# Wide bf16 products for TensorE in the idle times of a top-k search, and ahead of the first list and the first rows

## The chip, the cores and the metric

The kernel runs on one core of one Trainium2 chip. The metric is the device time of one execution in microseconds (us); the profile is one execution on that core. TensorE's granted clock has two levels in these rows, 1.2 GHz (shown as 0.50) and 2.4 GHz (1.00).

## The reference

An input of 16 x 512 tokens of 256 channels goes through four residual layers: a Mamba layer, a mixture of experts (MoE), linear attention, and the same MoE again. The change touches only the MoE:

```python
scores = (x_flat @ Wg.T).T                               # 8 experts x 8192 tokens
top_vals, token_idx = jax.lax.top_k(scores, capacity)    # capacity = 8192 / 8 = 1024
token_w = jax.nn.softmax(top_vals, axis=-1)
xg = x_flat[token_idx]
h = jax.nn.silu(jnp.einsum('eic,ehc->eih', xg, W1)) * jnp.einsum('eic,ehc->eih', xg, W3)
y = jnp.einsum('eih,ech->eic', h, W2) * token_w[..., None]
out = jnp.zeros_like(x_flat).at[token_idx.reshape(-1)].add(y.reshape(-1, c))
```

So each expert takes the 1024 tokens that score highest for it.

## The kernel before

`moe` is called twice, as stage `f` and as stage `g`; the tiles of a stage carry its letter in front. Stages follow one another: every engine waits for `done` before it starts the next one. Each engine executes its own instructions strictly in the order in which its function issues them.

**Search.** The 8 x 8192 scores lie as 128 partitions of 512 (16 partitions to an expert). The threshold of each expert is found bit by bit in `ROUNDS` = 15 rounds, each of which settles two bits. In a round, VectorE (`count_round`) compares all scores with `PAIR` = 3 trial thresholds (three instructions, L1685, each adding one to the semaphore `above`) and prepares the next round's patterns (L1687). TensorE (`totals_of`) waits for each comparison in turn and adds up over the 16 partitions of an expert with eight products of 64 columns (L1564), whose fixed operand is the 128 x 128 bf16 matrix `blk_b`; the 24 products of a round go to `tot`, the first bank of the PSUM tile `yp`. After the last one VectorE reduces `tot` (L1690), compares the counts with 1024 (L1693) and makes the next three thresholds (L1697). Nothing of one round overlaps the next: it is a chain comparison, products, reduction, threshold.

**First list.** After the search come two marks and a few small fp32 products (L1585, L1587, L1589), two scans, and a transposition of the positions (L1593). VectorE makes the one-hot tiles of expert 0 (`hots`, L1630, L1637, L1642; ScalarE makes one more, L1417), TensorE `compact(0)` turns them into a token list with 64 small bf16 products (L1486, into the first bank of `tp`), ScalarE copies the sums out (L1423), `add_parts(0)` adds them (L1500), and VectorE writes the list `tok` (L1646, L1648).

**First rows.** GpSimd gathers the 1024 rows of expert 0 with eight indirect DMAs (L1377), four to each half. `transposes(0, 0)` waits for the first four and transposes them into the second bank of `tp`, `transposes(0, 1)` uses the first bank (L1514); ScalarE copies each out (L1430). Then `hidden(0)` starts its fp32 products of 512 columns (L1536), and from there TensorE is nearly always busy to the end of the stage.

The second bank of `tp` (`tp[:, 1, :]`) is first used by `transposes(0, 0)`. `blk_b` is written before the search (L1657), and TensorE waits for it ahead of the first round (`one` at 2). TensorE's order around the change is

```python
for r in range(ROUNDS):
    totals_of(r)
...
nc.tensor.matmul(mrow[:, 0:NE], one[:, 0:P], ind_sw[:], start=True, stop=True).then_inc(S["sw"], 1)
compact(0)
add_parts(0)
transposes(0, 0)
transposes(0, 1)
for e in range(NE):
    hidden(e)
```

Of the kernel before, what the change touches and what calls it, by code (L numbers as in the profile page):

```python
# [21 lines left out]
P = 128  # L22
# [4 lines left out]
TJ = T // P  # L27
# [1206 lines left out]
def moe(nc, done, name, xn, res, scores, w, by_pool, turn, cleared):  # L1234
# [13 lines left out]
    with ExitStack() as stack:  # L1248
# [7 lines left out]
        blk_b = s.sb("blk_b", [P, P], BF16)  # L1256
# [64 lines left out]
        tp = s.ps("tp", [P, 2, T])  # L1321
# [153 lines left out]
        def tensor(pe):  # L1475
            def compact(e):


                pe.wait_ge(S["hot"], e + 1)
                pe.wait_ge(S["lval"], e + 1)  # L1480
                pe.wait_ge(S["lpart"], e + 1)
                if e:
                    pe.wait_ge(S["xev"], max(e - 2, 0) * 4 + 4)
                for n in range(COLS):
                    q = n % 4
                    last = nc.tensor.matmul(tp[q * SB:(q + 1) * SB, 0, 0:NV * SB], hot[:, :, n],  # L1486
                                            val[:, n, :, :].rearrange("p v m -> p (v m)"),
                                            start=n < 4, stop=n >= COLS - 4, skip_group_check=True)
                last.then_inc(S["cp"], 1)

            def add_parts(e):


                pe.wait_ge(S["ev"], e + 1)
                if e:
                    pe.wait_ge(S["tok"], e)
                else:
                    pe.wait_ge(S["fold"], 1)
                for q in range(4):
                    last = nc.tensor.matmul(slot[q * SB:(q + 1) * SB, :], fold[:],  # L1500
                                            sums[:, :, q * NSLOT:(q + 1) * NSLOT], start=True, stop=True,
                                            skip_group_check=True)
                last.then_inc(S["fd"], 1)

            def transposes(e, g):
                q, k, half = e % 2, g % 2, g // 2
                if k == 0:
                    pe.wait_ge(S[f"g{q}{half}"], g_base + 16 * TJ * (e // 2 + 1))
                if g >= 2 or e and (g == 0 or e + 1 == NE):
                    pe.wait_ge(S["xev"], e * 4 + g - 1)  # L1510
                elif g == 1:
                    pe.wait_ge(S["ev"], e + 2 if e else 1)
                for j in range(TJ):
                    last = nc.tensor.transpose(tp[:, 1 - g % 2, j * P:(j + 1) * P],  # L1514
                                               xg[:, q, half * TJ + j, k * P:(k + 1) * P], ident[:])
                last.then_inc(S["tr"], 1)
# [37 lines left out]
            def total_of(r):  # L1554
                pe.wait_ge(S["cnt"], r + 1)
                nc.tensor.matmul(tot[:, 0:1], blk[:], cnt[:], start=True, stop=True).then_inc(S["tot"], 1)

            def totals_of(r):


                for v in range(PAIR):
                    pe.wait_ge(S["above"], r * PAIR + v + 1)
                    for j in range(0, T, PART):
                        last = nc.tensor.matmul(tot[:, v * PART:(v + 1) * PART], blk_b[:], above[:, v, j:j + PART, 1],  # L1564
                                                start=j == 0, stop=j + PART == T, skip_group_check=True)
                last.then_inc(S["tot"], 1)
# [9 lines left out]
                             start=True, stop=True).then_inc(S["mcol"], 1)  # L1576
# [4 lines left out]
            pe.wait_ge(S["one"], 2)  # L1581
            for r in range(ROUNDS):
                totals_of(r)
            pe.wait_ge(S["above"], ROUNDS * PAIR + 2)
            nc.tensor.matmul(tot[:, 0:1], blk[:], cg[:], start=True, stop=True).then_inc(S["tot"], 1)  # L1585
            pe.wait_ge(S["ldc"], 16 * len(later))
# [8 lines left out]
            pe.wait_ge(S["isw"], 1)  # L1595
            nc.tensor.matmul(mrow[:, 0:NE], one[:, 0:P], ind_sw[:], start=True, stop=True).then_inc(S["sw"], 1)

            compact(0)
            add_parts(0)
            transposes(0, 0)  # L1600
            transposes(0, 1)
            for e in range(NE):
# [15 lines left out]
        def vector(dve):  # L1618
# [157 lines left out]
            for e in range(NE):  # L1776
# [16 lines left out]
                if e + 2 < NE:  # L1793
                    slots(e + 2)
        return Stage(s, sync, gpsimd, scalar, tensor, vector)


# [938 lines left out]
```

## Time and profile before

| | us |
|---|---|
| median of 3 runs | 3231.95 (3231.19 to 3232.04) |
| the profiled execution | 3231.11 |
| its span, first to last instruction | 3229.3 |
| TensorE busy in the span | 2691.7 |
| the search of stage `f`, of stage `g` | 1766.4 to 1810.3, 2769.5 to 2813.4 |
| first product of `hidden(0)`, `f` and `g` | 1840.68, 2843.31 |

The mean granted clock of TensorE over the span is 0.898 of full speed. The profiled execution ran 1.8 us longer than its span. Times in the rows count from the start of the span. A row of the timeline is one instruction or a merged run of like ones (x24): start, the time that they cover together, engine, line, operation, output and inputs, and in brackets how long the engine idled before and what released it. PEld is a load of the fixed operand ahead of a product.

### The profile page before, as it was taken

How to read it: one execution, taken by the hardware profiler on the slowest of the kernel's cores; microseconds unless marked ns; L12 is line 12 of the kernel's file. 1: busy time of each engine (PE TensorE's matmuls, PEld its weight loads, DVE VectorE, ACT ScalarE, POOL GpSimd, SP SyncE). 2: the span in 40 equal slices, each digit the busy share in tenths (PEclk: the TensorE clock that was granted, in tenths of full speed). 3: DMA queues.
4: the chain of work that ended last, by engine and by line, in shares of the span. 5: the costliest groups of instructions: out<-in, count | busy, mean ns of one | idle time of the engine just before them, and what ended most of it. 6: DMA issues, size and time to landing. Idle time of an engine off the chain costs nothing.

```text
span 3229.3 us, 46992 instructions
## 1 busy us (share of the span) xinstructions
PE 2691.7 (83%) x16734; PEld 1452.3 (45%) x16734; DVE 2230.9 (69%) x2386; ACT 1801.4 (56%) x3170; POOL 2086.6 (65%) x1301
## 2 busy tenths in 40 slices
PE   7788878887887788877855599996999999479998
PEld 3234233333333233323323355663777777345565
DVE  3999999999999999999997622211666666532211
ACT  4777778778877877777763122222555554022221
POOL 3899999999999999999994044543334343043453
PEclk9889899888899888988876599998999999589999
DMA  5556655665566555665562023432111111223342
GB/s 145 121 122 141 149 136 128 139 159 124 132 143 147 142 133 133 142 149 137 122 141 80 16 67 86 92 60 55 39 49 55 55 48 48 63 51 77 84 92 26
DMA packets 225478, 325.18 MB, mean 101 GB/s; under 512 B 40705, under 2 KB 116993, under 8 KB 225122
## 3 DMA queue, kind: packets, MB, share of 16 engines
q1 hardware_dynamic: 200674, 288.09, 36.1%
q0 software_dynamic: 24576, 34.10, 6.3%
q8 instruction: 138, 2.26, 0.3%
q14 instruction: 90, 0.74, 0.1%
HBM read 236.11 MB, written 85.98 MB: 100 GB/s over the span
## 4 chain that ended last, share of the span: by engine, by line
PE 52%; DVE 20%; issue 8%; POOL 7%; ACT 6%; DMA 5%; SPq 1%; another core or an unknown queue 1%; DVEq 0%; POOLq 0%; ACTq 0%
PE t_wb L2301 9%; PE m_wk L912 9%; PE g_h L1536 7%; PE f_h L1536 7%; DVE m_pair L789 6%; DVE m_hc L789 4%; DMA m_bc<-bcd 4%; PE m_y L1009 4%; DVE m_hc L798 4%; PE g_yp L1550 3%; PE f_yp L1550 3%; POOL m_side L698 3%; POOL m_hc L707 2%; PE t_a_ps L2301 2%; PE t_num L2301 2%
## 5 line engine op out<-in xcount | busy, mean ns | idle before, releaser
L698 POOL TENSOR_TENSOR m_side<-m_du_r,m_bc 128x1024 f32<-128x1024 f32 x384 | 901.1, 2363 | 9.6 <-DMA m_du_r<-ddd 9.6
L707 POOL TENSOR_TENSOR m_hc<-m_hc,m_bc 128x1024 f32<-128x1024 f32 x224 | 527.8, 2359 | 116.7 <-DVE m_hc L789 115.6
L434 ACT ACTIVATE m_pair<-m_delta_r,m_a_neg 128x512 f32<-128x512 f32 x768 | 497.9, 680 | 179.7 <-DVE m_hc L798 93.7
L789 DVE TENSOR_TENSOR_SCAN m_pair<-m_pair,m_side 128x1024 f32<-128x1024 f32 x224 | 511.5, 2283 | 20.3 <-ACT m_pair L434 16.9
L1009 PE MATMUL m_y<-m_hc,m_fold 128*32 128x512 f32 x2048 | 324.6, 709 | 203.5 <-DVE m_hc L798 145.2
L789 DVE TENSOR_TENSOR_SCAN m_hc<-m_pair,m_side 128x1024 f32<-128x1024 f32 x160 | 362.8, 2276 | 9.9 <-ACT m_pair L434 5.4
L798 DVE TENSOR_TENSOR m_hc<-m_pair,m_bc 128x1024 f32<-128x1024 f32 x288 | 350.6, 1217 | 5.7
L912 PE MATMUL m_wk<-m_xnT,m_w_in 128*128 128x512 f32 x488 | 293.4, 732 | 23.3 <-DVE m_delta L774 23.3
L912 PE MATMUL m_wk<-m_xs,m_cw_diag 128*128 128x512 f32 x480 | 226.8, 605 | 10.1 <-ACT m_xs L504 10.1
L1536 PE MATMUL g_h<-g_xgT,g_w 128*128 128x512 f32 x512 | 223.8, 597 | 0.8 <-issue 0.8
L1782 DVE TENSOR_TENSOR g_hT<-g_sg,g_h 128x512 f32<-128x512 f32 x64 | 44.0, 688 | 260.9 <-ACT g_sg L1445 260.9
L1782 DVE TENSOR_TENSOR f_hT<-f_sg,f_h 128x512 f32<-128x512 f32 x64 | 44.0, 688 | 260.6 <-ACT f_sg L1445 241.1
L1536 PE MATMUL f_h<-f_xgT,f_w 128*128 128x512 f32 x512 | 223.4, 596 | 0.8 <-ACT f_xgT L1430 0.8
L458 ACT ACTIVATE m_prod<-m_du_t,m_b_t 128x256 f32<-128x256 f32 x512 | 215.5, 496 | 3.1 <-PE m_pair L1065 2.2
L1009 PEld LDWEIGHTS m_y<-m_hc,m_fold 128*32 128x32 f32 x2048 | 45.6, 115 | 368.0 <-issue 367.9
L1377 POOL DMA_INDIRECT f_xg<-xn,f_tok x64 | 64.3, 1005 | 213.7 <-DVE f_tok L1648 196.7
L1377 POOL DMA_INDIRECT g_xg<-xn,g_tok x64 | 64.0, 1000 | 213.7 <-DVE g_tok L1648 196.6
L912 PEld LDWEIGHTS m_wk<-m_xnT,m_w_in 128*128 128x128 f32 x488 | 99.8, 227 | 217.3 <-issue 165.2
L789 DVE TENSOR_TENSOR_SCAN m_hc<-m_side,m_pair 128x1024 f32<-128x1024 f32 x64 | 146.0, 2282 | 38.2 <-issue 21.4
L434 ACT ACTIVATE m_side<-m_delta_r,m_a_neg 128x512 f32<-128x512 f32 x256 | 167.8, 711 | 0.0
L1065 PE MATMUL m_pair<-m_ident,m_prod 128*128 128x128 f32 x1024 | 139.7, 281 | 24.3 <-DVE m_hc L798 16.7
L1065 PEld LDWEIGHTS m_pair<-m_ident,m_prod 128*128 128x128 f32 x1024 | 120.6, 146 | 85.2 <-issue 85.2
(339 smaller groups left out, 4962.0 us busy)
## 6 DMA issues: line engine op xcount, KB each, us to landing
m_delta_r<-ddd SPq DMA_DIRECT2D x252, 256.0 KB, 6.6
m_du_r<-ddd SPq DMA_DIRECT2D x252, 256.0 KB, 7.5
m_bc<-bcd SPq DMA_DIRECT2D x192, 128.0 KB, 3.0
ddd<-m_delta SPq DMA_DIRECT2D x31, 512.0 KB, 3.0
ddd<-m_du SPq DMA_DIRECT2D x31, 512.0 KB, 3.8
f_w<-in_w SPq DMA_DIRECT2D x24, 512.0 KB
g_w<-in_w SPq DMA_DIRECT2D x24, 512.0 KB
m_xt<-in_x SPq DMA_DIRECT2D x16, 512.0 KB, 9.9
```

Of the source, the lines that this page charges most:

```text
L434: last = nc.scalar.activation(to, delta_r[:, c % 2, q, :], ACT.Exp, scale=a_neg[:, c * NQ + q, st:st + 1])
L458: last = nc.scalar.activation(prod[:, :, :, k, n * SB:(n + 1) * SB], du_t[:, k, :, :].rearrange("p c (h f d) -> p (c h) f d", h=2, d=SB), ...
L698: nc.gpsimd.tensor_tensor(side[:, un % RING, :, :], du_r[:, c % 2, 2 * h:2 * h + 2, :], bc[:, 0, st:st + 1, :].to_broadcast([P, 2, T]), AL ...
L707: nc.gpsimd.tensor_tensor(hc[:, un % RING, :, :], hc[:, un % RING, :, :], bc[:, 1, st:st + 1, :].to_broadcast([P, 2, T]), ALU.mult).then_i ...
L789: nc.vector.tensor_tensor_scan(to, decay, added, 0.0, ALU.mult, ALU.add).then_inc(S["scan"], 1)
L798: nc.vector.tensor_tensor(hc[:, un % RING, :, :], pair[:, un % 2, :].rearrange("p (i t) -> p i t", t=T), bc[:, 1, st:st + 1, :].to_broadca ...
L912: return nc.tensor.matmul(out, lhsT, rhs, start=first, stop=last)
L1009: last = nc.tensor.matmul(y[q * SB:(q + 1) * SB, c % 2, :], fold[:], hc[:, (2 * m + q // 2) % RING, q % 2, :], start=False, stop=st == NSE ...
L1065: last = nc.tensor.transpose(pair[:, un % 2, f * T + k * P:f * T + (k + 1) * P], prod[:, c % 2 * 2 + h, f, k, :], ident[:])
L1536: last = nc.tensor.matmul(out[:, m % 2, :], wt[:, q, k, f * P:(f + 1) * P], xgT[:, q, k, half * T:(half + 1) * T], start=k == 0, stop=k == ...
L1550: last = nc.tensor.matmul(yp[:, l % 2, 0:C], hT[:, half, f, j * P:(j + 1) * P], w2[:, e % 2, f, :], start=f == 0, stop=f == KF - 1)
L2301: return nc.tensor.matmul(out, lhsT, rhs, start=first, stop=last, **kw)
```

## The change

A function `unread(n)` is added to TensorE's part of `moe`. It issues n products of 512 columns in bf16: the fixed operand is `blk_b`, the moving operand is `blk_b` read four times over, and the output is the second bank of `tp`, which nothing reads before `transposes(0, 0)` overwrites it. No product waits for a semaphore or raises one. `unread(5)` follows the 24 products of each of the 15 rounds, `unread(12)` stands ahead of `compact(0)`, and `unread(16)` between `add_parts(0)` and `transposes(0, 0)`. That is 15 x 5 + 12 + 16 = 103 products in a stage, 206 in all. No other engine's instructions change.

```diff
+            def unread(n):
+                wide = blk_b[:].rearrange("p (o c) -> p o c", o=1).to_broadcast([P, TJ, P])
+                for _ in range(n):
+                    nc.tensor.matmul(tp[:, 1, :].rearrange("p (o c) -> p o c", c=P), blk_b[:], wide, start=True, stop=True)
+
             for r in range(ROUNDS):
                 totals_of(r)
+                unread(5)
...
+            unread(12)
             compact(0)
             add_parts(0)
+            unread(16)
             transposes(0, 0)
             transposes(0, 1)
```

## Rows read from the trace of the kernel before

**Rows 1.** Groups by line, the search: xcount | busy us, mean ns | idle before.

```profile
L1564 PE MATMUL f_yp<-f_junk,f_blk_b 128*128 128x64 bf16 x360 | 21.9, 242 | 20.1 <-DVE f_junk L1685 20.1
```

**Rows 2.** Timeline, one round of stage f.

```profile
1805.39 1.28 DVE L1685 TENSOR_SCALAR f_junk<-f_sc,f_trial 128x512 f32<-128x512 f32 x3
1805.93 1.30 PEld L1564 LDWEIGHTS f_yp<-f_junk,f_blk_b 128*128 128x128 bf16 x24 [1.59 <-DVE f_junk L1685]
1805.94 1.46 PE L1564 MATMUL f_yp<-f_junk,f_blk_b 128*128 128x64 bf16 x24 [1.43 <-DVE f_junk L1685]
...
1807.43 0.36 DVE L1690 TENSOR_REDUCE f_count<-f_yp 128x3 f32<-128x192 f32 x1 [0.69 <-PE f_yp L1564]
...
1808.28 1.28 DVE L1685 TENSOR_SCALAR f_junk<-f_sc,f_trial 128x512 f32<-128x512 f32 x3
```

**Rows 3.** Windows: length, busy us (count) by engine, granted clock, DMA share, GB/s.

```profile
core 0: us, PE busy (x) PEld busy (x) DVE busy (x) ACT busy (x) POOL busy (x), PEclk, DMA share, GB/s
452.00:461.00 9.00, 5.92 (x36) 2.81 (x36) 8.97 (x5) 7.54 (x14) 8.56 (x6) 1.00 0.31 117
461.00:470.00 9.00, 5.89 (x40) 2.87 (x44) 8.93 (x6) 6.37 (x12) 8.03 (x4) 1.00 0.78 193
...
478.50:481.80 3.30, 1.12 (x9) 0.31 (x10) 3.27 (x3) 2.58 (x6) 3.30 (x2) 1.00 0.26 66
482.00:485.20 3.20, 3.20 (x4) 0.68 (x2) 3.17 (x3) 2.36 (x5) 3.20 (x3) 0.50 0.45 142
...
1768.00:1810.00 42.00, 21.95 (x362) 19.68 (x361) 29.30 (x112) 0.58 (x1) 0.00 (x0) 0.50 0.22 53
1810.00:1820.00 10.00, 2.24 (x14) 1.92 (x12) 7.76 (x18) 0.00 (x0) 0.00 (x0) 0.50 0.00 0
...
1840.60:1843.90 3.30, 3.22 (x4) 1.51 (x5) 0.00 (x0) 1.24 (x1) 0.44 (x1) 0.50 0.26 73
1844.00:1855.00 11.00, 11.00 (x33) 5.39 (x32) 5.37 (x6) 3.45 (x6) 0.00 (x0) 1.00 0.00 0
...
2843.30:2847.20 3.90, 3.89 (x5) 1.82 (x6) 0.00 (x0) 1.16 (x1) 0.42 (x1) 0.50 0.22 62
```

**Rows 4.** One line, L1500: duration ns min/median/max, first and last start us.

```profile
L1500 PE MATMUL f_yp<-f_sums,f_fold x32: 182/183/196, 1829.3 to 2111.4; 128*32 128x16 bf16 x32
```

**Rows 5.** Timeline of stage f behind the search.

```profile
1812.65 0.59 PE L1585 MATMUL f_yp<-f_cg,f_blk 128*128 128x1 f32 x2 [2.36 <-DVE f_eq L1711]
...
1813.10 0.56 PE L1587 MATMUL f_h<-f_ce,f_low 128*128 128x1 f32 x2
...
1816.76 0.59 PE L1589 MATMUL f_h<-f_rows,f_low 128*128 128x1 f32 x2 [3.09 <-DVE f_sel L1723]
...
1819.65 1.11 PE L1593 MATMUL f_yp<-f_ident,f_pos 128*128 128x128 f32 x4 [2.30 <-DVE f_pos L1730]
...
1821.78 0.59 PE L1596 MATMUL f_yp<-f_ind_sw,f_one 128*128 128x8 f32 x2 [1.02 <-DVE f_ind_sw L1754]
...
1825.14 2.29 DVE L1642 TENSOR_TENSOR f_val<-f_lhot,f_tileb 128x2048 bf16<-128x2048 bf16 x1
...
1827.53 1.47 PE L1486 MATMUL f_tp<-f_val,f_hot 128*32 128x64 bf16 x64 [5.15 <-DVE f_val L1642]
...
1829.32 0.20 PE L1500 MATMUL f_yp<-f_sums,f_fold 128*32 128x16 bf16 x4 [0.32 <-ACT f_sums L1423]
...
1837.95 1.97 PE L1514 MATMUL f_tp<-f_ident,f_xg 128*128 128x128 f32 x8 [8.42 <-DMA f_xg<-xn,f_tok]
...
1840.68 8.69 PE L1536 MATMUL f_h<-f_xgT,f_w 128*128 128x512 f32 x16 [0.77 <-ACT f_xgT L1430]
```

**Rows 6.** Timeline, the same kinds of product at 2.4 GHz, later in stage f.

```profile
1860.47 1.66 PE L1486 MATMUL f_tp<-f_val,f_hot 128*32 128x64 bf16 x64
...
1877.01 0.66 PE L1514 MATMUL f_tp<-f_ident,f_xg 128*128 128x128 f32 x4 [1.96 <-DMA f_xg<-xn,f_tok]
```

**Rows 7.** Timeline, loads for `hidden(0)` as the clock rises.

```profile
1843.38 0.34 PEld L1536 LDWEIGHTS f_h<-f_xgT,f_w 128*128 128x128 f32 x1 [0.52 <-issue]
1844.06 0.19 PEld L1536 LDWEIGHTS f_h<-f_xgT,f_w 128*128 128x128 f32 x1 [0.34 <-issue]
1844.49 0.19 PEld L1536 LDWEIGHTS f_h<-f_xgT,f_w 128*128 128x128 f32 x1 [0.24 <-issue]
```

## The prediction

> **What bounds the kernel now.** I read the groups by line first, to see what TensorE does in the search. It is busy 21.9 us and idles 20.1 us, always until a comparison of VectorE is there [rows 1]. The timeline of one round comes next, because an average can't tell which half of the chain is late [rows 2]. A round lasts 2.89 us (1805.39 to 1808.28). The three comparisons take 1.28; TensorE starts 0.55 behind their start and ends at 2.01 (1807.40); VectorE then needs 0.88 for reduction and threshold before the next comparison. So TensorE's tail, 0.73 us from the end of the comparisons to the end of the products, lies on the path in each round, and VectorE waits 0.69 us for it. Third, the windows give the granted clock. Through the search, where TensorE is busy half the time, it is 0.50, that is 1.2 GHz; it stays there until `hidden(0)` has been dense for 3.3 us in stage f and 3.9 us in g, and is 1.00 behind [rows 3]. The 24 products are a queue at this clock: they cover 1.46 us, the last one alone takes 0.242, so they start every 0.053 us, which is 64 columns at 1.2 GHz. That is what can shrink. The added products compute nothing; their only possible gain is the clock.
>
> **A wide product's price.** None is in the trace. By the 0.053 us of 64 columns, 512 columns take eight times as long, 0.427 us at 1.2 GHz, and half of it, 0.213, at 2.4. Five take 2.13 or 1.07 us, twelve 5.12 or 2.56, sixteen 6.83 or 3.41.
>
> **Do they raise the clock?** In the first round they start behind the last small product, at about 1769.6, and at 1.2 GHz run to 1771.7. The next round's first comparison is there at 1771.2, so TensorE goes straight on, without a gap. This is the situation of the start of `hidden(0)`: dense work, and the clock up 3.3 and 3.9 us later [rows 3]. I expect the rise at 1772 to 1775, in the second or third round. **Do they hold it?** In a warm round TensorE works for 24 x 0.027 + 1.07 = 1.7 of 2.63 us, 65%, with one gap of 0.5 to 0.6 and two small ones. The stretch 452 to 470 of the Mamba stage is busy 11.8 of 18 us, 66%, with longer gaps, all at 1.00; a fall came behind 478.5 to 481.8, busy 1.12 of 3.30 [rows 3]. So I take it as held to the end of the search.
>
> **A warm round.** The third comparison is ready at 1.35 us after the round's start (comparisons start 0.40 apart, and TensorE follows 0.55 behind the first). The products of the first two are then out of the way, since eight take 8 x 0.027 = 0.21, under 0.40. The end is at 1.35 + 7 x 0.027 + the duration of one product. That duration is 0.242 cold. How much of it scales is bounded by the 16-column product, 0.196 in the cold stretch and 0.183 warm: nearly all of it is fixed, so 64 columns take 0.205 to 0.215 warm [rows 4]. End: 1.75 instead of 2.01, **0.26 us saved in a warm round**. The spacing of 0.027 is no row for a 128-column load with each product. Bounds: 0.053 (nothing changes) and 0.026, which the 64 products of `compact` show at 2.4 GHz (1.66 us) [rows 6]. I take the lower, as fp32 loads shorten with the clock, 0.34 to 0.19 us [rows 7]. The warm wide products end about 1.54 + 1.07 + 0.03 = 2.6 us after the round's start, and the next round's small ones are not due before 2.63 + 0.55 = 3.18: they are hidden, with 0.5 us of room.
>
> By the Trainium skill, "TensorE: Matmul & The Clock Gate", section on single matmul latency, an isolated product takes (219 + N)/1.2 ns cold and (398 + N)/2.4 ns warm, which for 64 columns is 236 and 192. The trace agrees with the first (242) and shows no second. As an estimate by that page a warm round would save 0.28 and the two stages together 0.5 us more than my sum.
>
> **The cold rounds.** There the cover fails. The five run to 1771.7 against 1771.2, so the second round ends 0.5 us late; if the clock has not risen in its wide products either, the third loses another 0.5, because 24 small and 5 wide ones take 1.28 + 2.13 = 3.41 us, more than 2.89. I take 0.5 with a quarter of a chance of 1.0, and a small chance of less if the rise comes early: 0.5. Sum for one search: 13 warm rounds x 0.26 = 3.4, less 0.5, is **2.9 us**; 12 rounds less 1.0 gives 2.1, 14 rounds with hardly a loss 3.5.
>
> **Behind the search.** The last five are done 1.1 us after the last small product, well ahead of L1585 (2.4 behind it). That product and L1587 take 1.0 us together at 1.2 GHz; if the clock is still up, 0.6 to 0.7. After that TensorE does 2.24 us of work in 10 [rows 3, 5], and the clock falls somewhere. Gain 0 to 0.8 (with L1589 and the four transpositions, 1.11 cold against 0.66 warm [rows 5, 6]); I take 0.3.
>
> **`unread(12)`** starts when L1596 is through, at 1822.25 in times of before. All cold it ends at 1827.4, and `compact(0)` is released at 1827.5 by VectorE [rows 5]: a cover with 0.1 us of room. If the clock rises on the way there is more. Cost 0 to 0.1; I take 0. `compact(0)` itself gains nothing from the clock: 64 products cover 1.47 us cold and 1.66 warm [rows 5, 6]. So this edit is worth -0.2 to 0, and I take 0.
>
> **`unread(16)`** starts at 1829.5 and ends at 1833.0 warm, 1836.4 cold; the rows are there at 1837.9 [rows 5]. It is hidden by the gather, with 1.5 us of room at least. Does its warmth reach the rows? Behind it TensorE idles 1.5 to 4.9 us. The stretch with 1.12 us of work in 3.3 was followed by a fall [rows 3], so in most phases the clock falls ahead of `hidden(0)` or within it. What is to be had: the transpositions, 1.97 us against at most 1.3 (twice the 0.66 of four), so 0.6 or more [rows 5, 6]; and four to five products of `hidden(0)` that ran at half speed for 3.3 and 3.9 us, that is 1.65 and 1.95 us. What is to be lost: a rise a little later than in this execution, up to 1.5. I take +0.3.
>
> **Sum.** 2.9 + 0.3 + 0 + 0.3 = 3.5 us a stage, 7.0 in all. Everything from `tok` on is a chain through gather and transpositions, and TensorE is dense behind it, so the gain isn't given back later. The profiled execution took 3231.11, 0.84 less than the median; so much is what two rises that come a little early or late make. Against it the sum gives 3224.1, against the median 3224.95. I forecast **3224.8 us**, a ratio of 0.998.
>
> **The rivals.**
> *Warm to the end of the gather* (R1): the clock is still up when `hidden(0)` starts, in both stages. For: the gap is only 1.5 us if `unread(16)` runs mostly cold. Against: if it does, it rose late, and warm it leaves 4.9. It adds 0.6 to 2.3 a stage: about 3221.
> *The rounds don't shorten* (R2): the clock rises, but a product with its 128-column load keeps starting every 0.053 us. For: no row shows such a pair warm. Against: loads scale in fp32 [rows 7]. The products then are a queue of 24 as before, and a round ends at 0.55 + 23 x 0.053 + 0.21 = 1.98 against 2.01: it saves 0.03 us, 0.4 a search, less 0.5, plus 0.6 behind it. Time 3231 to 3232, no change.
> *The clock does not rise, or not for long* (R3, the other side): the wide products then run at 1.2 GHz, each round becomes 24 small and 5 wide back to back, 3.41 us, and loses 0.52. In 14 rounds 7.3 us a stage: 3246. It decides as soon as more than 5 of 14 rounds are cold, for 5 x 0.52 = 2.6 then meets 9 x 0.26 = 2.3. For: these operands are bf16 with most values zero, and no dense stretch of such products is in the trace; the small ones ran half busy through 42 us without a rise. Against: both dense starts of `hidden(0)` and that of 482 to 485 ended in a rise [rows 3].
>
> **Chances.** Forecast 0.67 (its own range 3222.5 to 3227.5), R1 0.12, R2 0.12, R3 0.06, of which a partial one of 3230 to 3240 is half; 0.03 for anything else. The range of 8 in 10 takes in R1 and the lesser sizes towards R2: 3220.0 to 3230.0. A measurement of this kernel tells about 0.2%, 6.5 us, from no change; that line is at 3225.5, inside the forecast's own range. Two thirds of the forecast (0.44) and all of R1 lie beyond it: faster 0.56. Same 0.37, from the rest and R2. Slower 0.07.
>
> **What would show it.** In the windows of both searches the clock goes from 0.50 to 1.00 within 7 us and stays. A warm round in the timeline lasts 2.63 us, its 24 products cover 1.2, and VectorE waits 0.4 instead of 0.69. The second round, alone or with the third, is longer than 2.89. `compact(0)` starts right behind L1642, the first transposition waits for the gather's DMA and not for TensorE. If the rounds last 3.4, it is R3; if they last 2.87 at a clock of 1.00, R2; if `hidden(0)` shows no half-speed product, R1. I am wrong if the clock falls between rounds, or if `unread` stands in the way of `compact(0)` or of the rows.

## The result, and the profile after

The change takes **3223.8 us** (median of 14 runs, 3219.6 to 3226.4), the kernel before on the same chips 3231.36 (14 runs, 3229.7 to 3233.3). The ratio is 0.9977, 95% interval 0.9969 to 0.9984. Forecast were 3224.8 us (range 3220.0 to 3230.0) and a ratio of 0.998.

The groups by line, stage `f`, of the changed kernel (L1571 is L1564 of before, the small products; L1695 is L1685, a comparison; L1700 is L1690, VectorE's reduction; L1563 are the added products; idle time stands behind the second bar):

```profile
L1563 PE MATMUL f_tp<-f_blk_b 128*128 128x512 bf16 x103 | 28.6, 420 | 0.0
...
L1571 PE MATMUL f_yp<-f_junk,f_blk_b 128*128 128x64 bf16 x360 | 18.4, 199 | 4.6 <-DVE f_junk L1695 4.6
...
L1700 DVE TENSOR_REDUCE f_count<-f_yp 128x3 f32<-128x192 f32 x15 | 5.4, 357 | 8.7 <-PE f_yp L1571 8.7
```

The 360 small products took 242 ns each before [rows 1] and take 199 now, and TensorE idles 4.6 us ahead of them instead of 20.1. Being busier is no gain in itself; the gain is that VectorE's reduction waits 8.7 us in its 15 rounds. Before it waited 11.8: 0.69 in each round [rows 2] but the first, which cost 2.05 in both kernels, because TensorE still has four fp32 transpositions to do there.

Where the clock was, in stretches of stage `f` of the changed kernel (columns as in [rows 3]):

```profile
1771.00:1774.20 3.20, 3.20 (x30) 1.80 (x27) 2.09 (x8) 0.00 (x0) 0.00 (x0) 0.50 1.02 388
1774.40:1811.00 36.60, 31.08 (x392) 16.51 (x389) 29.09 (x111) 0.00 (x0) 0.00 (x0) 1.00 0.13 14
1811.00:1815.00 4.00, 0.61 (x4) 0.52 (x4) 3.34 (x8) 0.00 (x0) 0.00 (x0) 1.00 0.00 0
1815.20:1820.30 5.10, 1.79 (x8) 1.30 (x9) 4.13 (x12) 0.00 (x0) 0.00 (x0) 0.51 0.00 0
1820.30:1825.40 5.10, 5.10 (x13) 1.62 (x13) 5.07 (x3) 2.00 (x1) 0.00 (x0) 0.50 0.00 0
1825.60:1831.00 5.40, 5.08 (x84) 2.86 (x84) 0.33 (x2) 0.21 (x1) 1.85 (x2) 1.00 0.07 15
1831.00:1835.60 4.60, 0.06 (x1) 0.00 (x0) 2.63 (x6) 0.00 (x0) 3.38 (x5) 1.00 0.36 104
1835.80:1838.50 2.70, 1.97 (x8) 1.57 (x8) 0.00 (x0) 1.17 (x2) 2.09 (x3) 0.51 0.42 108
1838.60:1842.50 3.90, 3.88 (x5) 1.83 (x6) 0.00 (x0) 1.18 (x1) 0.43 (x1) 0.50 0.21 60
1842.70:1852.00 9.30, 9.30 (x29) 4.56 (x28) 4.71 (x4) 2.16 (x4) 0.00 (x0) 1.00 0.00 0
```

Read as a story: the search starts at 1.2 GHz; behind 3 us of dense work the clock is up, and it stays up to the end of the search. Behind it TensorE does 0.61 us of work in 4 and the clock falls. `unread(12)`, from 1820.3, runs at half speed, and the clock is up again just as it ends, at 1825.6. `unread(16)` runs at full speed and is done at 1831.0; TensorE idles 4.8 us, the clock falls at 1835.8, and the first rows arrive at 1835.9. So the transpositions and 4.0 us of `hidden(0)` run at half speed; before, it was the transpositions and 3.3 us. From the timeline:

```profile
1820.31 5.28 PE L1563 MATMUL f_tp<-f_blk_b 128*128 128x512 bf16 x12
...
1835.89 1.97 PE L1514 MATMUL f_tp<-f_ident,f_xg 128*128 128x128 f32 x8 [4.83 <-DMA f_xg<-xn,f_tok]
```

The first rounds and a later one, from the timeline of the changed kernel:

```profile
1770.02 1.49 PE L1571 MATMUL f_yp<-f_junk,f_blk_b 128*128 128x64 bf16 x24
...
1771.32 2.32 PE L1563 MATMUL f_tp<-f_blk_b 128*128 128x512 bf16 x5
...
1772.39 1.28 DVE L1695 TENSOR_SCALAR f_junk<-f_sc,f_trial 128x512 f32<-128x512 f32 x3
...
1773.44 1.31 PE L1571 MATMUL f_yp<-f_junk,f_blk_b 128*128 128x64 bf16 x24
...
1775.64 1.28 DVE L1695 TENSOR_SCALAR f_junk<-f_sc,f_trial 128x512 f32<-128x512 f32 x3
...
1799.34 1.28 DVE L1695 TENSOR_SCALAR f_junk<-f_sc,f_trial 128x512 f32<-128x512 f32 x3
...
1799.88 1.20 PE L1571 MATMUL f_yp<-f_junk,f_blk_b 128*128 128x64 bf16 x24 [0.35 <-DVE f_junk L1695]
...
1800.92 1.24 PE L1563 MATMUL f_tp<-f_blk_b 128*128 128x512 bf16 x5
1801.12 0.36 DVE L1700 TENSOR_REDUCE f_count<-f_yp 128x3 f32<-128x192 f32 x1 [0.43 <-PE f_yp L1571]
...
1801.97 1.28 DVE L1695 TENSOR_SCALAR f_junk<-f_sc,f_trial 128x512 f32<-128x512 f32 x3
```

In the second round the products start 1.05 us behind the comparison (1773.44 against 1772.39) instead of 0.55: the five wide ones at 1.2 GHz were in the way, and the round lasts 3.25 us (1772.39 to 1775.64). The warm round lasts 2.63 (1799.34 to 1801.97) instead of 2.89 [rows 2].

To compare kernels I cut each stage into six parts at instructions of its timeline and take differences of their starts. *Search*: first comparison to the first mark (L1710 of before). *Marks*: to the first ranks (L1738). *List*: to `tok` (L1648). *Gather*: to the first transposition. *Transp.*: to the first product of `hidden(0)`. *Hidden*: to the second step of VectorE's products there (L1782). Microseconds, stage f / stage g:

| kernel | search | marks | list | gather | transp. | hidden | sum |
|---|---|---|---|---|---|---|---|
| before | 44.74 / 44.75 | 9.63 / 9.62 | 8.98 / 8.96 | 8.17 / 7.73 | 2.73 / 2.74 | 9.36 / 9.80 | 83.61 / 83.60 |
| the change | 41.71 / 41.75 | 9.01 / 9.01 | 8.87 / 8.92 | 8.14 / 7.79 | 2.73 / 2.49 | 9.78 / 10.08 | 80.24 / 80.04 |

The change saves 3.37 and 3.56 us, 6.9 together, by this cut. The two spans differ by less, 4.8 us, mainly because what stands ahead of the first search, and is not changed, ran longer in that execution: the first comparison came at 1768.16 instead of 1766.43. A single span is no measure of a change of this size; the cut by stage and the medians are.

### The profile page after: what moved, and what is told of

Same layout as the page of the kernel before. It is cut to its first block, busy times and chain, and to the rows that moved or that the text cites. A ratio compares the mean times of both kernels' runs of the same rounds, so it can differ in the third digit from the quotient of the medians.

```text
span 3224.5 us, 47404 instructions
## 1 busy us (share of the span) xinstructions
PE 2735.5 (85%) x16940; PEld 1458.2 (45%) x16940; DVE 2230.9 (69%) x2386; ACT 1801.9 (56%) x3170; POOL 2086.3 (65%) x1301
## 4 chain that ended last, share of the span: by engine, by line
PE 52%; DVE 19%; issue 9%; POOL 7%; ACT 6%; DMA 5%; SPq 1%; another core or an unknown queue 1%; DVEq 0%; POOLq 0%; ACTq 0%
PE t_wb L2311 9%; PE m_wk L912 9%; PE g_h L1536 7%; PE f_h L1536 7%; DVE m_pair L789 6%; DVE m_hc L789 4%; DMA m_bc<-bcd 4%; PE m_y L1009 4%; DVE m_hc L798 4%; PE f_yp L1550 3%; PE g_yp L1550 3%; POOL m_side L698 3%; POOL m_hc L707 3%; PE t_a_ps L2311 2%; PE t_num L2311 2%
```

## The experiments

All ratios are to the kernel before on the same chip. The experiments ran on chips where it takes 3216 to 3218 us in place of 3231, so only ratios and the cut are compared. Lines shift by a few between these kernels; the comparison is L1693 in e3 and e4, and the small and the wide products keep L1571 and L1563.

| kernel | median us | ratio, 95% interval |
|---|---|---|
| e1_search_only | 3209.32 | 0.9977 (0.9968 to 0.9986) |
| e2_lists_only | 3216.67 | 0.9998 (0.9989 to 1.0008) |
| e3_two_wide | 3213.91 | 0.9991 (0.9982 to 1.0000) |
| e4_eight_wide | 3209.72 | 0.9978 (0.9968 to 0.9988) |
| e5_three_wide | 3209.91 | 0.9980 (0.9971 to 0.9989) |
| e6_thirty_four | 3204.67 | 0.9965 (0.9952 to 0.9979) |
| e7_gaps_filled | 3205.37 | 0.9965 (0.9952 to 0.9979) |
| e8_three_early_filled | 3204.73 | 0.9969 (0.9958 to 0.9981) |
| e9_change_again | 3209.69 | 0.9975 (0.9966 to 0.9984) |
| e10_early_then_five | 3201.74 | 0.9953 (0.9940 to 0.9967) |

| kernel | search | marks | list | transp. | hidden | sum |
|---|---|---|---|---|---|---|
| e1 | 41.54 / 41.23 | 9.13 / 9.21 | 8.96 / 8.93 | 2.74 / 2.73 | 9.59 / 9.56 | 80.06 / 79.41 |
| e2 | 44.74 / 44.73 | 9.62 / 9.62 | 8.96 / 8.89 | 2.73 / 2.37 | 10.51 / 10.20 | 84.71 / 83.50 |
| e3 | 42.15 / 42.95 | 9.62 / 9.62 | 8.94 / 8.96 | 2.73 / 2.73 | 10.15 / 9.23 | 81.79 / 81.23 |
| e4 | 42.23 / 42.36 | 9.21 / 9.21 | 8.96 / 8.93 | 2.73 / 2.74 | 9.22 / 9.50 | 80.48 / 80.43 |
| e5 | 41.10 / 41.10 | 9.20 / 9.61 | 8.96 / 8.93 | 2.74 / 2.74 | 9.20 / 9.31 | 79.35 / 79.46 |
| e6 | 41.89 / 41.76 | 9.20 / 9.01 | 8.97 / 8.89 | 1.91 / 1.91 | 7.78 / 7.77 | 77.94 / 77.11 |
| e7 | 41.54 / 41.12 | 8.55 / 8.54 | 8.91 / 8.93 | 1.92 / 1.92 | 7.77 / 7.77 | 76.90 / 76.04 |
| e8 | 41.10 / 41.10 | 8.75 / 8.75 | 8.94 / 8.94 | 1.92 / 1.91 | 7.77 / 7.77 | 76.60 / 76.19 |
| e9 | 41.59 / 41.86 | 9.10 / 9.21 | 8.92 / 8.91 | 2.73 / 2.49 | 9.73 / 10.07 | 80.01 / 80.28 |
| e10 | 41.10 / 41.11 | 8.55 / 8.55 | 10.06 / 8.90 | 1.91 / 1.91 | 7.77 / 7.77 | 77.57 / 76.03 |

(The gather is 7.7 to 8.2 us in every kernel and left out.)

### Which of the three places carries the gain

```diff
 e1_search_only, against the change
-            unread(12)
...
-            unread(16)
```

> Only the five products a round; the 12 and the 16 are left out. Theory: the gain is the shorter rounds of the search and a little behind it. Search of a stage (first comparison to the marks) 41.7 us as with the whole change (44.75 before), marks 9.0, list and gather as before; time 3224 to 3226, no more than 1 us from the whole change. Rival (the 12 and the 16 carry a warm clock to the list and the rows and share the gain): 3226 to 3228.

```diff
 e2_lists_only, against the change
-                unread(5)
```

> Only the 12 ahead of the first list and the 16 ahead of the first rows. Theory: both are hidden and bring nothing; search 44.75, list 8.9 to 9.0 us, the clock is back at 1.2 GHz for part of the transpositions and of hidden(0); time 3230 to 3232. Rival: a warm clock reaches hidden(0), 1.6 to 2.5 us a stage, 3226 to 3228.

The search alone gives the whole ratio, 0.9977; the 12 and the 16 alone give 0.9998, which is no measurable change. In e2 the search stays at 44.74 and 44.73. Its windows for stage `f` show the 12 and 16 working and their work lost (1.00 from 1824 to 1833, then 0.50 again as the rows come):

```profile
1824.00:1831.00 7.00, 5.29 (x85) 2.96 (x84) 1.16 (x3) 0.75 (x2) 2.18 (x2) 1.00 0.08 22
1831.00:1833.00 2.00, 0.00 (x0) 0.00 (x0) 1.71 (x4) 0.00 (x0) 1.66 (x2) 1.00 0.42 104
1834.00:1843.00 9.00, 6.93 (x14) 3.76 (x15) 0.00 (x0) 2.46 (x3) 3.50 (x4) 0.50 0.28 75
```

The hidden part is even longer, 10.51 and 10.20 us against 9.36 and 9.80. So two of the three edits of the change are worth nothing that can be measured, as sized.

### How many wide products a round needs

```diff
 e3_two_wide and e4_eight_wide, against e1_search_only
-                unread(5)
+                unread(2)    # e3; unread(8) in e4
```

> Two wide products a round in place of five, and no 12 and 16. At 1.2 GHz a round then has 1.28 + 0.85 = 2.13 us of work in 2.89, with an idle time of 0.7 us in each. Theory (the clock rises only behind dense work, and it is the clock that shortens the rounds): it stays at 0.50 through the search, rounds last 2.89, search 44.75, time 3230 to 3232. Rival (any more work in the idle time does it, without a late second round): the clock is 1.00, search 41.1, time 3224.

Both theories missed. The clock does rise with two, in the second round of both stages, but it doesn't stay. Windows of e3, stage `f`:

```profile
1770.00:1780.00 10.00, 6.36 (x104) 3.56 (x101) 7.84 (x32) 0.00 (x0) 0.00 (x0) 1.00 0.60 100
1780.50:1786.00 5.50, 4.50 (x52) 2.68 (x50) 3.90 (x16) 0.00 (x0) 0.00 (x0) 0.50 0.00 0
1787.00:1793.00 6.00, 4.00 (x66) 2.16 (x62) 4.52 (x17) 0.00 (x0) 0.00 (x0) 1.00 0.00 0
1794.00:1800.00 6.00, 4.79 (x56) 2.99 (x57) 4.39 (x17) 0.00 (x0) 0.00 (x0) 0.50 0.00 1
```

It goes up and down with the same instructions in each round, and the rounds follow it. Timeline of e3, a round in front of a rise and one behind it:

```profile
1782.71 1.28 DVE L1693 TENSOR_SCALAR f_junk<-f_sc,f_trial 128x512 f32<-128x512 f32 x3
1783.25 1.46 PE L1571 MATMUL f_yp<-f_junk,f_blk_b 128*128 128x64 bf16 x24 [0.57 <-DVE f_junk L1693]
...
1785.60 1.28 DVE L1693 TENSOR_SCALAR f_junk<-f_sc,f_trial 128x512 f32<-128x512 f32 x3
1786.15 1.20 PE L1571 MATMUL f_yp<-f_junk,f_blk_b 128*128 128x64 bf16 x24 [0.58 <-DVE f_junk L1693]
...
1788.24 1.28 DVE L1693 TENSOR_SCALAR f_junk<-f_sc,f_trial 128x512 f32<-128x512 f32 x3
```

At 1.2 GHz the round lasts 2.89 us and its 24 products cover 1.46; at 2.4 GHz it lasts 2.64 and they cover 1.20. The instructions are the same, so it is the clock that shortens a round, and not the mere presence of the wide products. My premise that only gapless work raises it was wrong: here it rose from rounds with an idle 0.6 us in each. The search gains 2.6 and 1.8 us, and the two stages differ by 0.8 with the same code.

> Eight wide products a round in place of five, and no 12 and 16. Theory: only the rounds before the clock rises pay, since eight at 1.2 GHz take 3.41 us; warm, they end 0.1 us behind the first comparison of the next round, which the slack of the first two comparisons takes up, so a warm round stays at 2.63. Search 42.5 to 43.5, time 3225.5 to 3228. Rival (a wide product that ends behind the first comparison costs its overhang in every round): search 44 to 45, time 3229 to 3231.

The theory held: with eight, a warm round is still 2.64 us (1790.43 to 1793.07), although its products start 0.68 us behind the comparison instead of 0.54. Timeline of e4:

```profile
1790.43 1.28 DVE L1693 TENSOR_SCALAR f_junk<-f_sc,f_trial 128x512 f32<-128x512 f32 x3
1791.11 1.07 PE L1571 MATMUL f_yp<-f_junk,f_blk_b 128*128 128x64 bf16 x24
1792.02 1.89 PE L1563 MATMUL f_tp<-f_blk_b 128*128 128x512 bf16 x8
...
1793.07 1.28 DVE L1693 TENSOR_SCALAR f_junk<-f_sc,f_trial 128x512 f32<-128x512 f32 x3
```

Only the products of the third comparison set the end, and they find TensorE free. What eight cost is the second round, with the clock still down (3.76 and 3.88 us): search 42.2 and 42.4 in place of 41.1 to 41.9 with five. That is 0.1 to 0.3 us under the lower end I had given; the ratio, 0.9978, can't tell eight from five.

```diff
 e5_three_wide, against e1_search_only
-                unread(5)
+                unread(3)
```

> Three wide products a round, and no 12 and 16. At 1.2 GHz a round has 1.28 + 1.28 = 2.56 us of work in 2.89, so that the next one's products are not late. Theory (three raise the clock and hold it, and the late second round of the change is saved): search 41.0 to 41.4 us in both stages, clock 1.00 from the second or third round to the end, 0.2 to 0.7 us less than with five; ratio to before 0.9973 to 0.998. Rival (three are like two, where the clock went up and down): search 42 to 43, clock falls between rounds, ratio 0.9985 to 0.999.

Of two, three, five and eight, three is the best size for the search: 41.10 us in both stages, the clock up from the second round and held, no round late. Windows of e5:

```profile
1772.00:1808.00 36.00, 25.52 (x372) 14.17 (x370) 28.42 (x111) 0.00 (x0) 0.00 (x0) 1.00 0.15 22
2756.00:2761.00 5.00, 3.93 (x33) 2.72 (x33) 2.78 (x12) 1.31 (x2) 0.00 (x0) 0.50 1.02 398
2762.00:2798.00 36.00, 25.17 (x365) 13.84 (x362) 28.46 (x111) 0.00 (x0) 0.00 (x0) 1.00 0.15 19
```

The change's 41.7 is 0.6 longer: the price of its second round, 3.25 and 3.28 us against 2.63. With five that price depends on when the clock rises: the second round of the other kernels with five lasts 2.65 (e7, stage `g`) to 3.41 us (e6, stage `f`). The ratios, 0.9980 in e5 and 0.9977 in e1 and in the change, can't tell these sizes apart.

### Why the 16 ahead of the first rows brought nothing

```diff
 e6_thirty_four, against the change
-            unread(16)
+            unread(34)
```

> The whole change with 34 wide products ahead of the first rows in place of 16. Theory (the clock fell because TensorE idled 4.8 us before the first rows): 34 take 7.3 us warm and end 1 us before the rows, the clock is 1.00 at the transpositions and in hidden(0); transpositions 2.1 us to the first product of hidden(0) instead of 2.5 to 2.7, the first two steps of hidden(0) 7.7 instead of 9.4 to 10.1; 2 to 2.5 us less a stage than the change, ratio 0.9960 to 0.9968. Rival (products for transpositions and hidden(0) start at half speed whatever runs before): no difference from the change, 0.9977. A third case: the 12 have not raised the clock, the 34 start cold and delay the rows, gather 1 to 4 us longer.

The theory held, by the cut and by the ratio, 0.9965. Timeline of TensorE in e6, stage `f`:

```profile
1825.51 7.51 PE L1563 MATMUL f_tp<-f_blk_b 128*128 128x512 bf16 x34
1834.02 1.09 PE L1514 MATMUL f_tp<-f_ident,f_xg 128*128 128x128 f32 x8 [1.00 <-DMA f_xg<-xn,f_tok]
1835.93 7.11 PE L1536 MATMUL f_h<-f_xgT,f_w 128*128 128x512 f32 x16 [0.82 <-ACT f_xgT L1430]
```

The eight transpositions cover 1.09 us instead of 1.97, and the 16 products of `hidden(0)` 7.11 instead of 8.69 [rows 5]. One number, an idle time of 1.0 instead of 4.8 us ahead of the rows, makes transpositions and hidden part 2.8 and 2.9 us shorter than in the change (9.69 and 9.68 against 12.51 and 12.57).

### Filling every gap

```diff
 e7_gaps_filled, against the change
 nc.tensor.matmul(offp[:, 0:1], low[:], ce[:], ...)
+            unread(10)
...
 nc.tensor.matmul(mcol[:, 0:1], low[:], rows[:], ...)
+            unread(7)
...
-            unread(12)
+            unread(22)
...
-            unread(16)
+            unread(34)
```

> The whole change, and TensorE filled at 2.4 GHz from the search on: 10 wide products behind L1595, 7 behind L1597, 22 ahead of the first list, 34 ahead of the first rows. Theory: the clock, up since the search, stays at 1.00 to the end of the stage; marks 8.4 us in place of 9.0, list 8.9, transpositions 2.1, first two steps of hidden(0) 7.7; 2.8 to 3.3 us less a stage than the change, ratio 0.9955 to 0.9962. Rival: the added ones stand in the way where each gap is short, marks 9.0 or more, and the gain over the change is under 2 us a stage.

From 1782 to 1855, in stage `f`, the clock is 1.00 in every window. The cut says 3.3 and 4.0 us less than the change, a little more than expected. The ratio, 0.9965, is above the range I gave (0.9955 to 0.9962), and it can't tell this kernel from e6.

```diff
 e8_three_early_filled, against e7_gaps_filled
+            pe.wait_ge(S["one"], 2)
+            unread(2)              # ahead of total_of(1)
...
+            unread(2)              # ahead of the transpositions of ex
...
-                unread(5)
+                unread(3)
```

> As e7_gaps_filled, but three wide products a round in place of five, and two each in two idle times ahead of the search. Theory: no round is late and the clock is up by the second round, so search 40.9 to 41.3, the rest as in e7; ratio 0.995 to 0.996, the fastest of all. Rival (three don't hold the clock): the search is 42 or more, the marks run cold, and the 22 and 34 at half speed delay list and rows; slower than e7 by over 2 us.

The search is 41.10, as expected. The two fillers ahead of it brought nothing of that: they raise the clock in the first round (1768.8, against 1771.6 in e5), but e5 without them has the same 41.10, since the first round lasts 4.24 us in every kernel. Marks are 8.75 instead of 8.55: with three a round the clock fell at 1810 and came back at 1813 under the filling. The ratio, 0.9969, is above the range I gave, and can't be told from those of e6 and e7.

### Both kernels against the best one, on one chip

```diff
 e10_early_then_five, against e8_three_early_filled
-                unread(3)
+                unread(3 if r < 2 else 5)
```

> The change itself, beside the next kernel on one chip. Theory: ratio to before 0.9977 as before; search 41.2 to 41.9, marks 9.0 to 9.2, transpositions 2.4 to 2.7, hidden(0) with 3 to 5 us at half speed.

> As e8_three_early_filled, but three wide products only in the first two rounds and five in the other 13. Theory: no late round, and the clock never falls behind the search: search 41.1, marks 8.55, list 8.9, transpositions 1.9, first two steps of hidden(0) 7.8, together 7 to 8 us less a stage than before; ratio 0.995 to 0.996, and 3 to 4 us a stage less than the change on the same chip. Rival (what is won in the first part of a stage is partly lost behind it, as the ratios of e6 to e8 can't tell apart): stage from the first comparison to the last scatter less than 6 us shorter, ratio 0.9965 or more.

The change repeats its ratio, 0.9975. e10 has 0.9953, 3201.74 us against 3209.69 on the same chip: 8.0 us less than the change, 16 less than before. It is faster than both; its slowest run, 3202.38, lies 5 us under the fastest of the change, 3207.59. From the first comparison to the start of the last scatter its stages take 434.4 and 432.8 us, e9's 436.7 and 437.1; the part behind the cut is the same within 0.1 (356.8 and 356.8 against 356.7 and 356.8), so nothing is given back. For stage `g` the expectation held (7.6 us less than before, 4.3 less than the change, a little more than I gave). For stage `f` it missed: the cut says 6.0 less than before, the stage is 2.3 shorter than that of the change, the list took 10.06 in place of 8.9, and the clock did fall behind the search.

Its stage `f` also shows a filler in the way, as one rival of e7 had it. Timeline of TensorE in e10, the same 22 products in `f` and in `g`, and below it the windows of `f`:

```profile
1816.11 6.59 PE L1563 MATMUL f_tp<-f_blk_b 128*128 128x512 bf16 x22
1822.64 1.56 PE L1486 MATMUL f_tp<-f_val,f_hot 128*32 128x64 bf16 x64
...
2804.23 4.91 PE L1563 MATMUL g_tp<-g_blk_b 128*128 128x512 bf16 x22
2809.74 1.42 PE L1486 MATMUL g_tp<-g_val,g_hot 128*32 128x64 bf16 x64 [0.60 <-DVE g_val L1656]
```

```profile
1807.00:1815.80 8.80, 5.36 (x27) 2.60 (x27) 7.43 (x22) 0.00 (x0) 0.00 (x0) 1.00 0.00 0
1816.30:1819.80 3.50, 3.50 (x10) 1.31 (x9) 3.47 (x3) 0.57 (x1) 0.00 (x0) 0.52 0.00 0
1819.90:1832.00 12.10, 11.80 (x115) 5.88 (x113) 4.57 (x9) 1.54 (x2) 4.76 (x5) 1.00 0.14 38
```

In `f` the clock fell at about 1816.4, behind a stretch of 8.8 us with 5.4 us of work, and the 22 took 6.59 us; `compact(0)` had no wait for VectorE and started late, and the list took 10.06 us instead of 8.90. This filler, sized for 2.4 GHz, cost 1.2 us because the clock dropped under it.

## Why the prediction was right, point by point

**The bound.** Right: the round's chain, with TensorE's tail at 1.2 GHz in it. e2, with the rounds untouched, has an unchanged search, and in e3 the length of the round goes with the clock.

**Rise and hold.** The rise was due 2.4 to 5.4 us behind the first wide product; it came 3.1 us behind it (1774.4 against 1771.3). It held through both searches, as the stretch of the Mamba stage suggested. The situation I took for the rise, work without a gap, was there, but e3 shows that it is not needed. R3, a clock that doesn't rise or not for long, was not seen with five or with three; with two it came true in part (e3).

**The warm round.** Forecast 2.63 us, measured 2.63; VectorE's wait 0.4 forecast, 0.43 measured. By the Trainium skill, "TensorE: Matmul & The Clock Gate", section on single matmul latency, a 64-column product takes 192 ns warm. The trace agrees, with a median of 192 for L1571, where I had taken 205 to 215. The estimate with that page's figure in my sum was 0.28 saved a round, the runs say 0.26. The difference to my working is in the spacing too: the products cover 1.20 us, of which 0.80 are the two comparisons and 0.19 the last product, so seven spacings are 0.21 us, 0.030 each instead of my 0.027. Two small errors cancel. R2, a spacing of 0.053, is ruled out by it.

**The cold rounds.** Forecast a loss of 0.5 us, measured 0.36 in stage `f` (3.25 against 2.89): the products of the second round were 0.5 late, but the clock rose while they ran (1.31 us instead of 1.46). The search gained 3.03 and 3.00; the sum said 2.9.

**Behind the search.** Forecast 0.3, measured 0.62 and 0.61. This term was mis-sized: the clock held until 1815.3, long enough for L1589 as well. VectorE waits 0.47 us for each of L1585 and L1589 instead of 0.68, and no longer 0.27 for L1587.

**`unread(12)`.** Forecast 0, with 0.1 us of room if it runs cold all the way. It did (5.28 us, done at 1825.6), `compact(0)` started 0.11 us behind the end of VectorE's last tile, against 0.10 before, and the list is 0.11 and 0.04 us shorter. Right, and right by little: e10 shows a filler at the same place that was too long once the clock fell.

**`unread(16)` and `hidden(0)`.** Forecast +0.3, measured -0.4 and 0.0 (transpositions and hidden part 12.09 and 12.54 before, 12.51 and 12.57 after). The mechanism was named, warmth that doesn't outlast the idle time, but the term has the wrong sign in stage `f`: the clock rose later within `hidden(0)` than before (4.0 us behind its first product instead of 3.3), the loss that I had allowed for and outweighed with a gain that did not come. R1 happened in neither stage. e6 shows what R1 needed: 18 products more.

**The sum.** 7.0 forecast, 6.9 by the cut, 7.6 by the medians. In each stage the two terms for the search and for what stands behind it were together 0.4 us too small, and the term for the 16 was 0.7 (`f`) and 0.3 (`g`) too large. The mechanism of the search was right; that the total came out this close is in part luck. That the gain is not given back behind the cut was right: from there to the start of the last scatter the stages take 363.9 and 363.8 us before and 362.5 and 363.9 with the change.

## What to carry to other kernels

If TensorE's short products lie on a chain with another engine, ask the windows which clock they run at; work that nobody reads, put into its waits, can be worth it. Size it twice: at the low clock it must not delay the next needed product by more than the warm rounds give back, and at the high clock it must reach so near to the next needed work that the clock is still up when that comes. Here an edit that warmed TensorE and then let it idle 4.8 us was worth nothing, and one that was sized for the high clock alone cost 1.2 us when the clock dropped.

## What the runs showed of the hardware that was not expected

- The clock rose without gapless work: with two wide products a round (e3) and 0.6 us of idle time in each, it was up in the second round, and then fell and rose again several times under the same instructions (1.00 to 1780, 0.50 to 1786, 1.00 to 1793). With three, five or eight it stayed to the end of the search.
- A fall came in e10 behind 8.8 us in which TensorE worked 5.4, in stage `f` and not in stage `g` of the same kernel, nor in e7, which has the same products at these places. Why there, with gaps that all of them share, is not settled.
- In a warm round of e4 the eight unneeded products in front of a chain of three groups cost nothing, though the first group starts 0.14 us late: only the last group is on the path.
- The 64 products of `compact(0)` cover 1.47 us cold [rows 5] and 1.42 at 2.4 GHz in stage `g` of e10; a later set of the same kind covers 1.66 at 2.4 GHz [rows 6]. The higher clock does almost nothing for them.
